# A fused attention and expert kernel: the projection of the batch three ahead moved half a step forward

## The chip, the cores and the metric

The kernel runs on one core of one Trainium2 chip. The metric is the device time of one execution in microseconds (us), lower is better.

## The reference

The input x is 16 batches of 256 tokens of 128 features. Two blocks follow each other, each added to its input:

```python
x = x + _layernorm(attention(_layernorm(x)))     # 16 heads of 8, causal, softmax
x = x + _layernorm(ffn(_layernorm(x)))           # 8 experts, one per token
# attention: Q,K,V = x @ W; softmax(Q K^T / sqrt(8), causal) V, then WO
# ffn: aff = x @ centroids.T; expert = argmax(aff); alpha = sigmoid(aff[expert])
#      y = x + relu(LN_e(x) @ w1_e.T + b1_e) @ w2_e.T + b2_e; out = alpha*y + (1-alpha)*x
```

## The kernel before, in words

The kernel is written by hand for five instruction streams (TensorE is PE, VectorE is DVE, ScalarE is ACT, GpSimd is POOL, and SyncE, called SP, only issues DMAs). Each stream has its own list of instructions in a fixed order, and semaphores order the streams against each other. An instruction that waits holds up all that stands behind it on its stream.

Three phases follow each other: a prologue (to about 38 us), the attention loop over batches (lines 252 to 255, `iterations`, steps 0 to 19 for 16 batches), and an expert phase over 39 tiles of sorted tokens (`tiles`, from about 340 us), which the change doesn't touch. The loop is a software pipeline. In step i these batches are worked on: `new` is i+3, `nxt` is i+1, `t` is i, `old` is i-1, and l2, l3, l4 (on ACT and PE `l2`, `ln`, `last`) are i-2, i-3, i-4. The last steps (i = 16 to 19) have no `t` any more and only drain the pipeline; step 15 has no `nxt`.

What is done for a batch, in its order:

- `normalise_x` (L651, ACT) writes the normalised rows xn; `transpose_x` (L783, PE) turns them into bank MA; `xnT_out` (L564, ACT) copies them out; `project_qk` (L791, PE) makes Q and K in bank MB.
- Q and K are split into three bf16 parts: `high` (L571, ACT) copies MB as bf16, `residue` (L1095, DVE) subtracts it, `middle` (L579, ACT) copies the residue as bf16, `low` (L429, POOL) subtracts that. `parts_out` (L301, SP) sends the parts (384 KB) to a buffer in DRAM, and `parts_in` (L309, SP) fetches them as six DMAs (768 KB) into `qaug` and `kaug`, in the layout that the scores need. A ring of three holds the batches.
- `scores_by_query` (L814, PE) computes the scores of 4 groups of heads (gr) in three portions each (u), into the two halves of bank S in turn, and `maxima` (L1102, DVE, the instruction at L1111) takes each row's maximum out of S. Portion n on PE waits until portion n-2's maximum is taken (the wait on `red`).
- `shift_parts` (L1119, DVE) splits the maxima of half of the heads into bf16 parts, `transpose_shift` (L807, PE) turns them (first half in MA, second in MB), `shift_out` (L584, ACT) copies them to nmT, and `shift` (L324, SP, the DMA at L330) writes them into two rows of qaug, 8 KB.
- In the batch's own step, `scores_near` and `scores_far` (L839, L851, PE) compute the scores again with the shift in them. `scores_near` of group 0 waits for the DMA of `shift(t, 0)`, of group 2 for `shift(t, 1)`. `exp_near` and `exp_far` (L603, L610, ACT) take the exponentials, `select` (L437, POOL) sets the upper triangle to zero, `weigh_values` (L860, PE) multiplies with V, which `project_v` (L799, PE, in MB) and `v_out` (L591, ACT) made.
- Later steps: `o_out`, `transpose_o` (MB), `divide`, `transpose_on`, `project_o`, `y_out`, the layer norm's statistics (`ln_stats`, `ln_aggregate`, `ln_variance` on DVE, `power` on POOL), `add_y`, then `transpose_f`, `affinities_and_ranks` (MB), `choose`, `count`, `place` on DVE, and `scatter` on POOL (L471), which writes the rows by indirect DMA into the experts' table. `add_y` of a batch waits until the scatter of the batch three before has landed (L1198).

MA and MB are each one PSUM bank: the next user on PE waits for the readers of the last one (`take_m`).

The DMAs of SP share one queue. Its order in step i is: `shift(i,1)`, `parts_out(i+2)`, `parts_in(i+2)`, `shift(i+1,0)`, and in some steps a load of expert weights.

Of the kernel before, what the change touches and what calls it, by code (L numbers as in the profile page):

```python
# [51 lines left out]
def sandwich_kernel(nc, x, attn_w, w1x, w2t, b2, cent_t, out):  # L52
# [31 lines left out]
    with ExitStack() as ctx:  # L84
# [209 lines left out]
        def _(sp):  # L294
# [46 lines left out]
            shift(Nth(0), 0)  # L341

            def step(i):
                if b := at(i, 0):
                    shift(b, 1)
                if b := at(i, 2):
                    parts_out(b)
                if b := at(i, 2):
                    parts_in(b)
                if b := at(i, 1):  # L350
                    shift(b, 0)

# [56 lines left out]
        def _(pool):  # L409
# [99 lines left out]
            def step(i):  # L509
                t, ln, last = at(i, 0), at(i, -2), at(i, -4)  # L510
# [5 lines left out]
                if t:  # L516
                    select(t, 2)
                if t:
                    select(t, 3)
                if last:  # L520
                    scatter(last, 0)
                if ln:
                    power(ln, 1)
                if last:
                    scatter(last, 1)
                if ln:
# [3 lines left out]
                if b := at(i, 3):  # L530
                    low(b)
# [29 lines left out]
        def _(act):  # L561
# [109 lines left out]
            middle(Nth(2))  # L671

            def step(i):
# [10 lines left out]
                if new:  # L684
                    normalise_x(new)
                if ln:
                    fT_out(ln)
                if t:
                    exp_near(t, 1)
                    exp_far(t, 1)  # L690
                if new:
                    xnT_out(new)
                if t:
                    exp_near(t, 2)
                if ln or last:
                    affinities_and_ranks_out(i.plus(-3), ln, last)
                if t:
                    exp_far(t, 2)
                if nxt:
                    shift_out(nxt, 0)  # L700
                if nxt:
                    v_out(nxt)
                if t:
                    exp_near(t, 3)
                if old:
                    onT_out(old)
                if t:
                    exp_far(t, 3)
                if new:
                    high(new)  # L710
                if ln:
                    exp_negative(ln)
                if new:
                    middle(new)
# [60 lines left out]
        def _(pe):  # L775
# [176 lines left out]
            def step(i):  # L952
                t, new, nxt, old, l2, ln, last = (at(i, n) for n in (0, 3, 1, -1, -2, -3, -4))

                for gr in range(NG):
# [6 lines left out]
                    if gr == 1 and old:  # L962
                        transpose_o(old)
                    if gr == 2 and i.k == 1:
                        centroid_sums()
                    if gr == 2 and (ln or last):
                        affinities_and_ranks(i.plus(-3), ln, last)
                    if gr == 3 and old:
                        transpose_on(old)
                    if t:  # L970
                        scores_far(t, gr)
                    if nxt:
# [9 lines left out]
                    if gr == 2 and nxt:  # L982
                        transpose_shift(nxt, 0)
                    if gr == 3 and new:
                        project_qk(new)
                    if nxt:
                        scores_by_query(nxt, gr, 2)
                    if gr == 1 and new:
                        transpose_x(new)
# [540 lines left out]
```

## Time and profile before

| what | us |
|---|---|
| median of 3 runs | 438.01 |
| lowest and highest of them | 433.75, 443.32 |
| the profiled execution | 438.63 |
| its span, first to last instruction | 436.9 |

The rows below come from the profiled execution. Times are from its span's start. Step i of the loop is counted from the first `scores_near` of its batch on PE: step 0 begins at 38.52 us, step 1 at 55.45, step 2 at 71.76, step 3 at 91.20, step 4 at 109.03, step 10 at 214.35, step 11 at 231.56, step 14 at 282.05, step 15 at 298.12.

### The profile page before, as it was taken

How to read it: one execution, taken by the hardware profiler on the slowest of the kernel's cores; microseconds unless marked ns; L12 is line 12 of the kernel's file. 1: busy time of each engine (PE TensorE's matmuls, PEld its weight loads, DVE VectorE, ACT ScalarE, POOL GpSimd, SP SyncE). 2: the span in 40 equal slices, each digit the busy share in tenths (PEclk: the TensorE clock that was granted, in tenths of full speed). 3: DMA queues.
4: the chain of work that ended last, by engine and by line, in shares of the span. 5: the costliest groups of instructions: out<-in, count | busy, mean ns of one | idle time of the engine just before them, and what ended most of it. 6: DMA issues, size and time to landing. Idle time of an engine off the chain costs nothing.

```text
span 436.9 us, 11197 instructions
## 1 busy us (share of the span) xinstructions
PE 334.4 (77%) x3642; PEld 268.4 (61%) x3642; DVE 335.6 (77%) x1215; ACT 243.9 (56%) x574; POOL 244.4 (56%) x337
## 2 busy tenths in 40 slices
PE   2348699868978988869897798698620799999950
PEld 1226566656866766647676576485420799999950
DVE  7848777849889799586897898786744399999980
ACT  2204456555765765546667566466410598888850
POOL 3823253625564764654647557547564058888883
PEclk9998989989999999898999999899855699999995
DMA  7662854737536436154363463602004566777710
GB/s 216 107 106 46 113 118 56 110 64 99 86 60 91 93 48 108 51 80 84 49 110 87 52 104 74 90 9 88 14 20 131 160 176 167 205 196 187 217 39 6
DMA packets 34681, 42.78 MB, mean 98 GB/s; under 512 B 5465, under 2 KB 25053, under 8 KB 33088
## 3 DMA queue, kind: packets, MB, share of 16 engines
q1 hardware_dynamic: 31744, 37.43, 44.3%
q0 software_dynamic: 2304, 4.37, 3.1%
q8 instruction: 30, 0.49, 0.5%
q10 hardware_dynamic: 576, 0.27, 0.2%
q14 instruction: 27, 0.22, 0.2%
HBM read 30.59 MB, written 11.66 MB: 97 GB/s over the span
## 4 chain that ended last, share of the span: by engine, by line
PE 44%; DMA 29%; DVE 12%; POOL 5%; issue 5%; ACT 2%; SPq 2%; POOLq 0%; DVEq 0%; ACTq 0%
DMA aug<-nmT 21%; PE ST L848 5%; PE S L1016 4%; PE O L869 4%; PE ST L1016 3%; PE O L1029 3%; PE S L835 3%; PE MB L1029 3%; DVE nmf L1111 3%; PE S L825 2%; PE S L828 2%; DMA qk_parts<-qkp 2%; DMA xs_rows<-pay,pos 2%; PE S L830 2%; DMA aug<-qk_parts 2%
## 5 line engine op out<-in xcount | busy, mean ns | idle before, releaser
L1111 DVE TENSOR_REDUCE nmf<-S 128x2 f32<-128x512 f32 (+1 forms) x192 | 129.5, 681 | 52.3 <-PE S L828 28.3
L441 POOL TENSOR_SCALAR_AFFINE_SELECT p<-p 128x512 f32<-128x512 f32 x64 | 40.9, 638 | 82.5 <-ACT p L608 82.5
L608 ACT ACTIVATE p<-ST 128x1024 f32<-128x1024 f32 x64 | 65.4, 1021 | 26.0 <-PE ST L848 25.2
L848 PE MATMUL ST<-aug 128*128 128x256 bf16 x256 | 40.4, 282 | 30.2 <-DMA aug<-nmT 30.2
L835 PE MATMUL S<-aug 126*128 126x128 bf16 x512 | 51.3, 223 | 0.0
L471 POOL DMA_INDIRECT xs_rows<-pay,pos x32 | 33.1, 1033 | 29.0 <-DVE pos L1270 25.2
L539 POOL DMA_INDIRECT out_x<-vaug,x_all x39 | 42.5, 1090 | 7.8 <-issue 7.5
L848 PEld LDWEIGHTS ST<-aug 128*128 128x128 bf16 x256 | 23.6, 100 | 35.3 <-DMA aug<-nmT 32.6
L445 POOL TENSOR_SCALAR_AFFINE_SELECT p<-p 128x512 f32<-128x512 f32 x64 | 41.2, 644 | 7.1 <-ACT p L612 4.4
L869 PE MATMUL O<-p,vaug 128*32 128x256 f32 x512 | 41.5, 394 | 1.4 <-POOL p L441 1.4
L835 PEld LDWEIGHTS S<-aug 126*128 126x128 bf16 x512 | 40.9, 100 | 2.4
L830 PE MATMUL S<-causal,identb 128*128 128x256 bf16 x128 | 36.4, 284 | 6.9 <-DVE nmf L1111 6.2
L612 ACT ACTIVATE p<-ST 128x512 f32<-128x512 f32 x64 | 38.3, 599 | 0.3
L549 POOL TENSOR_TENSOR rsz<-vez,mhalf 128x1 f32<-128x1 f32 x39 | 22.1, 567 | 24.8 <-DVE vez L1463 24.2
L1434 DVE TENSOR_SCALAR vaug<-ST,w1s 128x128 f32<-128x128 f32 x78 | 23.5, 341 | 11.5 <-PE ST L1016 11.3
L825 PE MATMUL S<-causal,identb 128*128 128x512 bf16 x64 | 25.8, 403 | 7.4 <-DMA aug<-qk_parts 7.4
L435 POOL TENSOR_TENSOR qkp<-res,qkp 128x512 bf16<-128x512 f32 x16 | 18.6, 1163 | 19.7 <-ACT qkp L582 19.7
L1016 PE MATMUL S<-vaug,w1s 128*128 128x128 f32 x156 | 25.5, 288 | 1.6 <-DMA w1s<-in_w1x 0.6
L828 PEld LDWEIGHTS S<-aug 126*128 126x128 bf16 x256 | 20.9, 102 | 9.5 <-issue 1.9
L828 PE MATMUL S<-aug 126*128 126x128 bf16 x256 | 26.3, 227 | 0.0
L873 PE MATMUL O<-p,vaug 128*32 128x128 f32 x512 | 26.2, 275 | 0.0
L577 ACT ACTIVATE qkp<-MB 128x512 bf16<-128x512 f32 x16 | 9.6, 597 | 29.4 <-PE MB L795 29.4
(163 smaller groups left out, 871.7 us busy)
## 6 DMA issues: line engine op xcount, KB each, us to landing
w1s<-in_w1x SPq DMA_DIRECT2D x39, 259.0 KB, 3.2
qk_parts<-qkp SPq DMA_DIRECT2D x16, 384.0 KB, 2.8
aug<-qk_parts SPq DMA_DIRECT2D x32, 192.0 KB
aug<-qk_parts SPq DMA_DIRECT2D x32, 128.0 KB
x_all<-xs_rows SPq DMA_DIRECT2D x39, 67.0 KB, 2.3
aug<-qk_parts SPq DMA_DIRECT2D x32, 64.0 KB
w_tab<-in_w2t SPq DMA_DIRECT2D x8, 256.0 KB, 6.0
out_x<-vaug,x_all POOLq DMA_INDIRECT x39, 3.1
```

The lines of the kernel that those rows point to most:

```text
L441: g.affine_select(out=v, in_=v, compare_op=ALU.is_ge, fill=0.0, base=0, pattern=[[0, 4], [1, P]], channel_multiplier=-1).then_inc(s["sel0" ...
L445: g.affine_select(out=v, in_=v, compare_op=ALU.is_ge, fill=0.0, base=0, pattern=[[0, 4], [1, P]], channel_multiplier=-1).then_inc(s["sel1" ...
L539: g.indirect_dma_start(out=out.rearrange("b t d -> (b t) d"), out_offset=bass.IndirectOffsetOnAxis(ap=xs[:, q, TOK:TOK + 1].bitcast(U32), ...
L608: a.activation(p0[:, gr % 2], ST0[:, :, :], ACT.Exp, scale=SCALE).then_inc(s["exp0"], 1)
L612: a.activation(p1[:, gr % 2], ST1[:, :, :], ACT.Exp, scale=SCALE).then_inc(s["exp1"], 1)
L828: last = mm(bank[:, j * P:(j + 1) * P], q[:, h, 0:P], k[:, h, 0:P], start=False, stop=(j == 3))
L830: mm(bank.rearrange("p (j c n) -> p j c n", j=2, c=2)[:, :, 1], identb[:, :], causal[:, 0:2], start=True, stop=False)
L835: last = mm(bank[:, j * SEQ + kb * P:j * SEQ + (kb + 1) * P], q[:, h, P:SEQ], k[:, h, kb * P:(kb + 1) * P], start=False, stop=(j == 1 and ...
L848: last = mm(ST0[:, j], kaug[:, p, h, 0:P], qaug[:, p, h], start=True, stop=True)
L869: mm(O[32 * j:32 * j + 32, gr // 2, :], vaug[:, p, 0, 4 * gr + j], p0[:, odd, j], start=not odd, stop=False)
L1016: last = mm(hidden(p, c), w1s[:, t.slot(WR), c * P:(c + 1) * P], nT[:, p], start=True, stop=True)
L1111: v.tensor_reduce(dst, S[:, n % 2].rearrange("p (j n) -> p j n", j=k), op=ALU.max, axis=AX_X, negate=True).then_inc(s["red"], 1)
```

## The change

On all five streams the work for `new` is placed earlier:

- SP: `parts_out` is now for i+3 and stands last in the step, behind `shift(i+1,0)`; `parts_in(i+2)` follows `shift(i,1)` directly.
- ACT: `normalise_x` for batch i+4 stands at the end of the step (and one for batch 3 ahead of the loop). `high(new)` stands before `exp_far(t,2)`, `middle(new)` before `exp_near(t,3)`, `v_out(nxt)` just before `exp_far(t,3)`; `affinities_and_ranks_out` is earlier.
- PE: `affinities_and_ranks` moves from group 2 to group 1, `transpose_x` to an earlier place in group 1, `transpose_o` to a later one, `transpose_shift(nxt,0)` and `project_qk(new)` to the front of group 2, `project_v(nxt)` to the end of group 3.
- DVE: `divide` moves behind `shift_parts(nxt,0)`, `residue(new)` ahead of maximum (3,0), `place` and `alphas` are earlier (`place(l4,2)` follows `add_y`), `choose(l3,1)` and `count(l3,0)` are placed anew.
- POOL: `low(new)` stands between `select(t,2)` and `select(t,3)`; `scatter(last,0)` before it, and `scatter(last,1)` ahead of `power(ln,1)`.

```diff
@@ SP
             shift(Nth(0), 0)
+            parts_out(Nth(2))
 
             def step(i):
                 if b := at(i, 0):
                     shift(b, 1)
                 if b := at(i, 2):
-                    parts_out(b)
-                if b := at(i, 2):
                     parts_in(b)
                 if b := at(i, 1):
                     shift(b, 0)
+                if b := at(i, 3):
+                    parts_out(b)
@@ POOL
                 if t:
                     select(t, 2)
+                if last:
+                    scatter(last, 0)
+                if new:
+                    low(new)
                 if t:
                     select(t, 3)
                 if last:
-                    scatter(last, 0)
+                    scatter(last, 1)
                 if ln:
                     power(ln, 1)
-                if last:
-                    scatter(last, 1)
-                if ln:
                     number(ln)
                 if i.k < 2:
                     power_x(i.k + 3)
-                if b := at(i, 3):
-                    low(b)
@@ ACT
             middle(Nth(2))
+            normalise_x(Nth(RING))
...
-                if new:
-                    normalise_x(new)
                 if ln:
                     fT_out(ln)
                 if t:
                     exp_near(t, 1)
-                    exp_far(t, 1)
+                if ln or last:
+                    affinities_and_ranks_out(i.plus(-3), ln, last)
                 if new:
                     xnT_out(new)
                 if t:
+                    exp_far(t, 1)
                     exp_near(t, 2)
-                if ln or last:
-                    affinities_and_ranks_out(i.plus(-3), ln, last)
+                if nxt:
+                    shift_out(nxt, 0)
+                if new:
+                    high(new)
                 if t:
                     exp_far(t, 2)
-                if nxt:
-                    shift_out(nxt, 0)
-                if nxt:
-                    v_out(nxt)
+                if new:
+                    middle(new)
                 if t:
                     exp_near(t, 3)
                 if old:
                     onT_out(old)
+                if nxt:
+                    v_out(nxt)
                 if t:
                     exp_far(t, 3)
-                if new:
-                    high(new)
                 if ln:
                     exp_negative(ln)
-                if new:
-                    middle(new)
+                if b := at(i, 4):
+                    normalise_x(b)
@@ PE
-                    if gr == 1 and old:
-                        transpose_o(old)
-                    if gr == 2 and i.k == 1:
+                    if gr == 1 and i.k == 1:
                         centroid_sums()
-                    if gr == 2 and (ln or last):
+                    if gr == 1 and (ln or last):
                         affinities_and_ranks(i.plus(-3), ln, last)
+                    if gr == 2 and nxt:
+                        transpose_shift(nxt, 0)
+                    if gr == 2 and new:
+                        project_qk(new)
                     if gr == 3 and old:
                         transpose_on(old)
                     if t:
                         scores_far(t, gr)
+                    if gr == 1 and new:
+                        transpose_x(new)
...
-                    if gr == 2 and nxt:
-                        transpose_shift(nxt, 0)
-                    if gr == 3 and new:
-                        project_qk(new)
+                    if gr == 1 and old:
+                        transpose_o(old)
                     if nxt:
                         scores_by_query(nxt, gr, 2)
-                    if gr == 1 and new:
-                        transpose_x(new)
-                    if gr == 2 and nxt:
+                    if gr == 3 and nxt:
                         project_v(nxt)
@@ DVE
+                if l4:
+                    alphas(l4, 0)
                 if nxt:
                     maxima_and_stats(i, nxt, 1, 1)
                 if l2:
                     ln_variance(l2, 0)
                 if l4:
-                    alphas(l4, 0)
+                    alphas(l4, 1)
...
+                if nxt:
+                    maxima_and_stats(i, nxt, 1, 2)
+                if l4:
+                    place(l4, 0)
+                if nxt:
+                    shift_parts(nxt, 0)
                 if old:
                     divide(old)
-                if l4:
-                    alphas(l4, 1)
-                if nxt:
-                    maxima_and_stats(i, nxt, 1, 2)
                 if nxt:
                     maxima_and_stats(i, nxt, 2, 0)
-                    shift_parts(nxt, 0)
+                if l4:
+                    place(l4, 1)
+                if l3:
+                    choose(l3, 0)
                 if l2:
                     add_y(l2)
+                if l4:
+                    place(l4, 2)
...
+                if new:
+                    residue(new)
                 if nxt:
                     maxima_and_stats(i, nxt, 3, 0)
...
-                if new:
-                    residue(new)
+                if l3:
+                    count(l3, 0)
                 if nxt:
                     shift_parts(nxt, 1)
```

## Rows read from the trace of the kernel before

**Rows 1.** Busy time by stretch: PE, PEld, DVE, ACT, POOL; PE clock, DMA share, GB/s.

```profile
55.45:282.05 226.60, 194.71 (x2392) 148.69 (x2393) 185.12 (x587) 138.54 (x297) 125.76 (x173) 0.97 0.49 82
176.50:196.33 19.83, 15.98 (x186) 12.34 (x187) 14.29 (x47) 11.01 (x24) 11.29 (x16) 0.93 0.41 68
214.35:231.56 17.21, 14.72 (x186) 11.26 (x187) 15.19 (x52) 11.45 (x25) 10.93 (x15) 1.00 0.48 83
282.05:298.12 16.07, 14.92 (x181) 11.48 (x182) 12.30 (x40) 9.08 (x19) 7.38 (x12) 0.90 0.08 24
```

**Rows 2.** Waits of the whole run: total us, times, longest.

```profile
PE ST L848 <- DMA aug<-nmT: 30.2, 14, 3.9
```

**Rows 3.** Timeline of SP in step 10: start us, us.

```profile
216.97 0.62 SPq L330 DMA_DIRECT2D aug<-nmT  x1
218.00 0.39 SPq L307 DMA_DIRECT2D qk_parts<-qkp  x1
221.01 0.31 SPq L318 DMA_DIRECT2D aug<-qk_parts  x1
...
224.44 0.62 SPq L330 DMA_DIRECT2D aug<-nmT  x1
```

**Rows 4.** The chain of waits at the same place.

```profile
224.44 7.07 DMA aug<-nmT
```

**Rows 5.** Timeline of PE, end of step 10 and start of step 11.

```profile
228.96 0.39 PE L835 MATMUL S<-aug 126*128 126x128 bf16 x4
231.56 0.61 PE L848 MATMUL ST<-aug 128*128 128x256 bf16 x4 [2.21 <-DMA aug<-nmT]
```

**Rows 6.** Timeline of DVE in step 10: divide, maxima, residue.

```profile
221.50 0.42 DVE L1138 TENSOR_TENSOR on<-MB,rden 128x256 f32<-128x256 f32 x1
...
221.91 1.27 DVE L1111 TENSOR_REDUCE nmf<-S 128x2 f32<-128x512 f32 x2
...
228.09 0.68 DVE L1111 TENSOR_REDUCE nmf<-S 128x4 f32<-128x512 f32 x1
...
230.12 0.67 DVE L1099 TENSOR_TENSOR res<-MB,qkp 128x512 f32<-128x512 f32 x1
```

**Rows 7.** Timeline of ACT in step 10: normalise_x, v_out, middle.

```profile
217.85 0.87 ACT L658 ACTIVATE xn<-x_all,nbx,rsx 128x128 f32<-128x128 f32 x2
...
225.09 0.45 ACT L600 ACTIVATE vaug<-MB 128x128 f32<-128x128 f32 x2 [0.67 <-PE MB L802]
...
230.82 0.63 ACT L582 ACTIVATE qkp<-res 128x512 bf16<-128x512 f32 x1 [1.08 <-DVE res L1099]
```

**Rows 8.** Groups of instructions, steps 4 to 13: busy us, mean ns.

```profile
L608 ACT ACTIVATE p<-ST 128x1024 f32<-128x1024 f32 x40 | 40.9, 1021 | 9.2 <-PE ST L848 8.7
...
L1187 DVE TENSOR_SCALAR pay<-mv_x 128x2 f32<-128x2 f32 x10 | 5.3, 528 | 0.0
...
L1188 DVE TENSOR_SCALAR ve_x<-mv_x 128x2 f32<-128x2 f32 x10 | 1.6, 155 | 0.0
```

**Rows 9.** Timeline of DVE and SP in step 0.

```profile
39.75 0.16 DVE L1084 SCALAR_TENSOR_TENSOR nbx<-mvx,rsx 128x6 f32<-128x6 f32 x1
...
44.30 0.31 SPq L318 DMA_DIRECT2D aug<-qk_parts  x1
```

**Rows 10.** The chain of waits in steps 16 and 17.

```profile
313.95 0.62 DVE pay L1200 x2
...
316.22 0.74 issue
316.96 1.04 POOL xs_rows L471
318.03 1.04 POOL pay L454
319.08 0.20 issue
...
321.72 0.63 DVE pay L1200 x2
```

More of the change, by code:

```diff
@@ L509, in step @@
             def step(i):
-                t, ln, last = at(i, 0), at(i, -2), at(i, -4)
+                t, new, ln, last = at(i, 0), at(i, 3), at(i, -2), at(i, -4)
                 if t:
@@ L1325, in step @@
                 if l4:
-                    alphas(l4, 0)
+                    alphas(l4, 1)
+                if i.k == 1:
+                    centre_centroids()
+                if nxt:
[4 more added lines that the diff above has]
+                    shift_parts(nxt, 0)
                 if old:
                     divide(old)
-                if l4:
-                    alphas(l4, 1)
-                if nxt:
-                    maxima_and_stats(i, nxt, 1, 2)
                 if nxt:
                     maxima_and_stats(i, nxt, 2, 0)
-                    shift_parts(nxt, 0)
+                if l4:
+                    place(l4, 1)
+                if l3:
+                    choose(l3, 0)
                 if l2:
                     add_y(l2)
+                if l4:
+                    place(l4, 2)
                 if nxt:
@@ L1341, in step @@
                     ln_stats(l2, 1)
-                if l4:
-                    place(l4, 0)
-                if i.k == 1:
-                    centre_centroids()
                 if l3:
-                    choose(l3, 0)
+                    choose(l3, 1)
                     ln_shift(l3)
@@ L1352, in step @@
                     maxima_and_stats(i, nxt, 2, 2)
-                if l4:
-                    place(l4, 1)
                 if l3:
-                    choose(l3, 1)
                     scale_max(l3)
@@ L1359, in step @@
                     ln_variance(l2, 1)
+                if new:
+                    residue(new)
                 if nxt:
                     maxima_and_stats(i, nxt, 3, 0)
-                if l4:
-                    place(l4, 2)
                 if l3:
@@ L1376, in step @@
                 if l3:
-                    count(l3, 0)
                     count(l3, 1)
```

## The prediction

> **What bounds the kernel now.** I read the busy time by stretch first, then the waits, then one step in the timeline of each engine, and last the chain of waits. The loop's steps 1 to 13 (55.45 to 282.05 us) take 226.6 us, 17.43 each. In them PE is busy 194.7 and DVE 185.1, which is 15.0 and 14.2 a step, so neither fills its step; but the engines are near enough to each other that removing one wait uncovers the next [rows 1]. PE's largest wait is that of the first `scores_near` of a step for the DMA that writes the shift: 30.2 us in 14 times [rows 2]. Step 10 shows why it is late. `shift(i,1)` is issued 2.6 us into the step (216.97 against 214.35), `parts_out` at 218.00, and `parts_in` stands behind its landing until 221.01 [rows 3]. `shift(i+1,0)` is issued at 224.44, is 8 KB, and takes 7.07 us, since the 768 KB of `parts_in` are ahead of it [rows 3, 4]. PE has done its own step at 228.96 + 0.39 = 229.35, 15.0 us after the start, and stands still for 2.21 until 231.56 [rows 5]. So in such a step PE and DVE have some 15 us of work and the DMA queue sets 17.2. Where a transfer runs late the step grows one for one: the step of 176.50 took 19.83 [rows 1].
>
> **The DMA side of the change.** `parts_out(i+2)` goes a step back, so `parts_in` follows `shift(i,1)` directly. From the first issue of `parts_in` to the landing of the shift behind it is 231.51 - 221.01 = 10.5 us [rows 3, 4]. ACT reaches `shift_out(t,1)` later than now, because `v_out` (0.45), `exp_far(3)` (some 0.5) and `normalise_x` (0.87) now stand between the step's start and `exp_near(0)` [rows 7], 1.5 to 1.8 together; I put the shift's issue at 4.2 us into the step instead of 2.6. `parts_in` then starts at about 4.8, and the shift has landed at 4.8 + 10.5 = 15.3. PE needs it at 16 to 17. The wait is hidden with 1 to 2 us to spare, and a slow transfer like that of the 19.83 us step is mostly absorbed. `parts_out` itself (one DMA, the same count as before) takes 3.0 us to land (218.00 to 221.01) [rows 3]; issued near 0.5 of the next step, after POOL's `low`, it lands at 3.5, ahead of the point (4.8) where `parts_in` waits for it. The shift it stands ahead of, `shift(i,1)`, is issued at 4.2 and needed at 7.
>
> The Trainium skill ("DMA: Bandwidth & Descriptors", Queues, rings and completion order) says that each DMA engine takes descriptors in ring order but that completion isn't first-in first-out for one issuing engine. Were a small DMA free to overtake, the wait before the change would not be behind `parts_in` at all and moving it would give nothing in this term; the 7.07 us of an 8 KB transfer speak for the ring order [rows 4].
>
> **What is late next: DVE's stretch between two maxima.** PE may run only two portions ahead of DVE, so the order on DVE decides. Before, from the start of maximum (1,2) to that of (3,0) DVE needs 228.09 - 221.91 = 6.18 us without a gap [rows 6]. Into this stretch the change puts `divide` (reciprocal and product, start to start some 0.8, of which the product is the 0.42 at 221.50) and `residue` (0.67) [rows 6]: 7.6, with a small `place` 7.7. Portion (1,2) is ready at about 7.9 into the step (before 7.56, by 221.91 - 214.35 [rows 5, 6]): PE has `affinities_and_ranks` and `transpose_x` ahead of it, and the former waits for `fT_out` on ACT, some 0.4. The residue is then ready at 15.6. ACT has `middle` (0.63) [rows 7] and `exp_near(3)` (1.02) [rows 8] behind it, and the next step's `scores_near` waits for that exponential: 15.6 + 0.6 + 1.0 + 0.1 = 17.3. That is the upper bound of the step by this order. PE's own stops beside it (`transpose_shift` waits for `shift_parts` some 0.6, `project_qk` for `divide` another 0.6, since both now stand early in group 2) lie inside it.
>
> The lower bound comes from DVE instructions that are stretched now. The same small operation takes 0.528 at L1187 and 0.155 at L1188 [rows 8]; in the stretch counted above four kinds do this (variance, one-hot, `add_y`, the cast of the shift), together about 1.5 us. They are the ones that meet a select on POOL. In the new order POOL has its selects of group 2 done before the variance comes, so part of this goes: 15.8 if all goes. I take 16.7, a little nearer to the order's sum than to the other end, because the one-hot still meets a select.
>
> The Trainium skill ("SBUF — State Buffer", Who interferes with whom) has VectorE and GpSimd share a port pair under an exclusive lock held for a whole instruction. By that rule the loss depends on which instructions meet, not on their number; with none meeting the step would be 15.8 and the whole about 412, with all of them 17.3 and about 431. The trace agrees in kind: 0.528 beside 0.155 [rows 8].
>
> **The sum, against the profiled execution's 438.6 us.**
>
> - Start of the loop: `normalise_x(3)` now stands ahead of `exp_near(0,0)` on ACT and waits for DVE's bias at 39.75 [rows 9], and takes 0.87 [rows 7, 9], so that exponential and `shift(0,1)` behind it come some 1.7 later, the DMA at 42.5; `parts_in(2)`, whose parts have by then landed, still starts at 43.2 instead of 44.30 [rows 9]. Step 1 begins 1.1 us sooner.
> - Steps 1 to 13: 13 x (17.43 - 16.7) = 9.5 us less [rows 1]. Of the 30.2 us of waits this keeps a third; the rest turns into waits of PE for DVE and ACT. In it is the clock: in the step of 176.50 to 196.33 the granted clock is 0.93 and PE's same 186 instructions take 15.98 instead of 14.72 [rows 1]. It falls to the lower of its two levels (1.2 of 2.4 GHz) after such a stop; with stops under 1 us I count none.
> - Step 14 (16.07 us, clock 0.90 [rows 1]) loses its slow start but is held by DVE: 0.3 less.
> - The drain (steps 15 to 19). The chain goes from `add_y` to its next 321.72 - 313.95 = 7.77 us later: `add_y`, statistics and choosing up to `pos`, scatter 1.04, `power` 1.04 with 0.20 behind it, second scatter, landing [rows 10]. `place(l4,2)` now follows `add_y` directly, which lets the first scatter start 1.4 sooner (313.95 + 0.62 + 0.16 + 0.74 = 315.5 against 316.96), and `power` no longer stands between the scatters, 1.24. That is 2.7 for the link shown. The one before has only the 1.2 of `power`; in the last one the chain needs `power` itself, which now stands behind two scatters, so that of the 1.4 only 0.2 is kept. Together 4.1. Between 0 (if y's own path ends last) and 5.5 (two full links).
> - The expert phase and the work ahead of 38.5 us: nothing changes, 0.
>
> 438.6 - 1.1 - 9.5 - 0.3 - 4.1 = 423.6 us. The profiled execution is 0.6 above the median of the runs, so the two stand for the same kernel; single runs of it spread by 2%.
>
> What I cost at nothing: the earlier `alphas` and `count` (DVE waits there for PE anyway, in groups 0 and 1), the move of `transpose_x`, and SP's extra `parts_out` ahead of the loop (its three us are inside step 0).
>
> **Rivals.**
>
> *PE becomes the bound.* If DVE runs less tightly than I count, the step falls to PE's own 15.0 [rows 5] and some 0.3: 15.3. Then 13 x 2.13 = 27.7, and 438.6 - 1.1 - 27.7 - 0.3 - 4.1 = 405. For it: PE is busy 14.72 in a clean step. Against: DVE is busy 15.19 there [rows 1]. Chance 0.12.
>
> *The stretched instructions stay, or the gain is only the late transfers.* Step 17.2: 13 x 0.23 = 3, and 438.6 - 1.1 - 3 - 0.3 - 4.1 = 430. For it: the sum in order gives 17.3. Chance 0.22.
>
> *The fetch doesn't come sooner (the change doesn't do what it says).* `low(new)` now stands behind `scatter(last,0)` on POOL, which waits for `place` on DVE; if `parts_out` lands after 7 us of the step, `parts_in` starts when it does now. Then only the start's slack and the drain count: 438.6 - 4.1 = 434.5. Against: POOL is busy 10.93 of 17.21 [rows 1]. Chance 0.08.
>
> *Slower: ACT's order closes the loop.* ACT is in order, and `middle(new)` waits for DVE ahead of `exp_near(3)`, `v_out` waits for the last product of PE's step ahead of `exp_far(3)`, and both stand ahead of the next `exp_near(0)`. `exp_near(0)` starts 2.0 into the step (0.2 until the product is there, then the 1.5 to 1.8 from above) and ends at 3.0; PE asks for it (group 1) at 3.5. If `v_out` starts over 0.5 us later than I have it, every us more on ACT is a us more on the step. With 1 us over my upper bound the step is 18.3: 13 x 0.87 = 11.3 more, 438.6 - 1.1 + 11.3 - 4.1 = 444.7. It decides from a step of 17.8 on, where the drain's gain is used up. Against: ACT is busy 11.45 of 17.21 [rows 1]. Chance 0.10.
>
> **How the numbers follow.** The forecast (step 15.8 to 17.0, which is 412 to 428) has 0.48, the rivals 0.12, 0.22, 0.08 and 0.10. The range runs from 411 to 435: below it is the rival with PE as the bound, above it the slower one. A measurement of this kernel can tell about 2% from no change, that is 429 on the one side and 447 on the other. The forecast and PE's rival fall under 429, and of the 430 case a little less than half: 0.70 faster. Same: the rest of it, the late fetch and most of the slower case: 0.25. Slower by over 2%: 0.05.
>
> **What would show it.** In the changed profile: PE's wait at `scores_near` for the DMA of nmT falls from 30.2 us to under 5; SP issues `parts_in` 4 to 5.5 us into a step, not 6.7; new waits of PE at `transpose_shift` for DVE and at `project_qk` for `divide`, 0.3 to 0.8 each; ACT's `middle` directly behind DVE's `residue`, with `exp_near(3)` behind it; the granted clock 0.98 and more over steps 1 to 13, none as long as 19.83; in the drain the two scatters side by side and `add_y` to `add_y` 5 to 5.5 us. Wrong would be: a wait of `scores_near` for the DMA of over 1 us a step, a step with PE at 15.3, or one over 17.8.

## The result, and the profile after

| what | before | after |
|---|---|---|
| median, us | 436.28 (4 runs) | 413.51 (4 runs) |
| lowest and highest | 433.75, 443.32 | 412.54, 414.44 |
| the profiled execution | 438.63 | 413.59 |
| its span | 436.9 | 411.8 |

The ratio is 0.9496, with a 95% interval of 0.9429 to 0.9563: the change makes the kernel 5% faster. From profile to profile it gives 25.0 us, where 15.0 were forecast. The time lies inside the range, 10 us below the forecast. Some executions are slower as a whole, at a lower granted clock (the profiled one of before, 443.32 before, 448.62 of fetch_late, 496.48 of both_moves), and by the others alone, as in all ratios here, the change is worth 21.9 us rather than 25.0.

Busy time by stretch after the change (columns as in [rows 1]): steps 1 to 13, step 9, and step 14.

```profile
52.78:259.81 207.03, 191.67 (x2392) 146.63 (x2393) 176.54 (x599) 131.57 (x294) 122.94 (x172) 1.00 0.52 92
196.40:212.48 16.08, 14.98 (x186) 11.49 (x187) 13.74 (x48) 10.39 (x25) 9.99 (x15) 1.00 0.50 84
259.81:275.01 15.20, 13.91 (x183) 10.48 (x180) 13.54 (x47) 8.62 (x19) 8.83 (x13) 1.00 0.10 29
```

The 13 steps take 19.57 us less [rows 1], and the granted clock is 1.00 in all of them, instead of 0.97. They are alike now: steps 3 to 12 take 16.1 each, where [rows 1] show one of 19.83 and one of 17.21 (step 13, the first without `new`, takes 15.15). The start of step 1 came forward from 55.45 to 52.78 (2.67), step 14 is 0.87 shorter, and from the start of step 15 to the expert phase's first normalisation on ACT it is 40.10 instead of 41.75 (1.65). These four are 24.8 of the 25.0.

Waits: PE's for the DMA of the shift over the whole run, and PE's two largest in 84 to 244 us (ten steps).

```profile
PE ST L849 <- DMA aug<-nmT: 0.5, 1, 0.5
PE MB L796 <- DVE on L1139: 4.2, 10, 0.4
PE MA L811 <- DVE nmp L1129: 4.1, 10, 0.4
```

The wait of [rows 2] went from 30.2 us in 14 times to 0.5 in 1. What came instead is 0.42 and 0.41 a step. SP's timeline, from step 9 (196.40) to step 10 (212.48), answers to [rows 3]:

```profile
199.99 0.62 SPq L330 DMA_DIRECT2D aug<-nmT  x1
200.70 0.38 SPq L318 DMA_DIRECT2D aug<-qk_parts  x1
...
205.88 0.62 SPq L330 DMA_DIRECT2D aug<-nmT  x1
212.70 0.39 SPq L307 DMA_DIRECT2D qk_parts<-qkp  x1
216.07 0.62 SPq L330 DMA_DIRECT2D aug<-nmT  x1
```

`shift(9,1)` is issued 3.6 us into its step, `parts_in` 4.3, and `parts_out` 0.2 into the next step. PE no longer stands at the end of a step (compare [rows 5]):

```profile
211.42 0.28 PE L831 MATMUL S<-causal,identb 128*128 128x256 bf16 x1
...
211.76 0.66 PE L803 MATMUL MB<-wat,xnT 128*128 128x128 f32 x4
212.48 0.60 PE L849 MATMUL ST<-aug 128*128 128x256 bf16 x4
```

DVE's stretch of the same step, from maximum (1,2) to the residue (compare [rows 6]):

```profile
204.08 0.69 DVE L1112 TENSOR_REDUCE nmf<-S 128x2 f32<-128x512 f32 x1 [0.87 <-PE S L836]
...
207.70 0.69 DVE L1112 TENSOR_REDUCE nmf<-S 128x2 f32<-128x512 f32 x1 [0.43 <-PE S L836]
...
208.70 0.38 DVE L1215 SCALAR_TENSOR_TENSOR hotk<-aff,amax,down 128x8 f32<-128x8 f32 x2
...
209.88 0.25 DVE L1188 TENSOR_SCALAR pay<-mv_x 128x2 f32<-128x2 f32 x1
...
210.09 0.68 DVE L1100 TENSOR_TENSOR res<-MB,qkp 128x512 f32<-128x512 f32 x1
210.69 0.68 DVE L1112 TENSOR_REDUCE nmf<-S 128x4 f32<-128x512 f32 x1
...
211.96 0.75 DVE L1222 TENSOR_TENSOR hot<-down,key 128x16 bf16<-128x16 f32 x1
```

The maximum starts 7.68 into the step, and the residue is done 6.69 later, at 210.77, which is 14.37. Of the 6.69, 0.43 is DVE standing still for PE's portion (2,1) at 207.70, so 6.26 is its own work. ACT follows it without a gap, and `exp_near(3)` ends at 212.33, 0.15 before PE begins the next step:

```profile
210.80 0.63 ACT L582 ACTIVATE qkp<-res 128x512 bf16<-128x512 f32 x1 [2.57 <-DVE res L1100]
211.33 1.00 ACT L608 ACTIVATE p<-ST 128x1024 f32<-128x1024 f32 x1
```

### The profile page after: what moved, and what is told of

The parts are those of the page before. It is cut to its first block, busy times and chain, and to the rows that moved or that the text cites. A ratio compares the mean times of both kernels' runs of the same rounds, so it can differ in the third digit from the quotient of the medians.

```text
span 411.8 us, 11210 instructions
## 1 busy us (share of the span) xinstructions
PE 331.5 (80%) x3642; PEld 265.7 (65%) x3642; DVE 326.3 (79%) x1215; ACT 237.3 (58%) x574; POOL 241.3 (59%) x337
## 4 chain that ended last, share of the span: by engine, by line
PE 44%; DVE 21%; issue 12%; POOL 8%; DMA 7%; ACT 4%; SPq 2%; POOLq 0%; DVEq 0%; ACTq 0%
PE S L836 5%; DVE nmf L1112 5%; PE O L870 4%; PE MB L796 4%; POOL out_x L539 3%; PE ST L849 3%; PE S L831 3%; PE MB L884 2%; PE ST L858 2%; DVE res L1100 2%; DMA aug<-qk_parts 2%; PE O L874 2%; PE S L1017 2%; POOL rsz L549 2%; PE S L829 2%
## 5 line engine op out<-in xcount | busy, mean ns | idle before, releaser
L446 POOL TENSOR_SCALAR_AFFINE_SELECT p<-p 128x512 f32<-128x512 f32 x64 | 40.7, 636 | 42.9 <-ACT p L612 42.4
L442 POOL TENSOR_SCALAR_AFFINE_SELECT p<-p 128x512 f32<-128x512 f32 x64 | 40.5, 633 | 28.7 <-ACT p L608 28.6
L836 PE MATMUL S<-aug 126*128 126x128 bf16 x512 | 50.6, 221 | 0.0
L836 PEld LDWEIGHTS S<-aug 126*128 126x128 bf16 x512 | 40.3, 99 | 2.1
L472 POOL DMA_INDIRECT xs_rows<-pay,pos x32 | 32.2, 1005 | 14.2 <-DVE pay L1257 6.5
L849 PE MATMUL ST<-aug 128*128 128x256 bf16 x256 | 38.5, 272 | 1.9 <-ACT p L608 0.7
L582 ACT ACTIVATE qkp<-res 128x512 bf16<-128x512 f32 x16 | 10.1, 630 | 35.0 <-DVE res L1100 35.0
L829 PEld LDWEIGHTS S<-aug 126*128 126x128 bf16 x256 | 20.3, 99 | 9.0 <-issue 1.1
L849 PEld LDWEIGHTS ST<-aug 128*128 128x128 bf16 x256 | 21.9, 97 | 5.9 <-issue 2.2
L796 PE MATMUL MB<-xnT,wat 128*128 128x256 f32 x64 | 20.8, 454 | 6.1 <-DVE on L1139 5.0
```

The source lines that it names most:

```text
L442: g.affine_select(out=v, in_=v, compare_op=ALU.is_ge, fill=0.0, base=0, pattern=[[0, 4], [1, P]], channel_multiplier=-1).then_inc(s["sel0" ...
L446: g.affine_select(out=v, in_=v, compare_op=ALU.is_ge, fill=0.0, base=0, pattern=[[0, 4], [1, P]], channel_multiplier=-1).then_inc(s["sel1" ...
L796: last = mm(MB[:, w * SEQ:(w + 1) * SEQ], wat[:, w], xnT[:, b.slot(RING)], start=True, stop=True)
L836: last = mm(bank[:, j * SEQ + kb * P:j * SEQ + (kb + 1) * P], q[:, h, P:SEQ], k[:, h, kb * P:(kb + 1) * P], start=False, stop=(j == 1 and ...
L849: last = mm(ST0[:, j], kaug[:, p, h, 0:P], qaug[:, p, h], start=True, stop=True)
```

## The experiments

My theory after the result: the queue no longer sets the step. The step is set by the chain residue, `middle`, `exp_near(3)`, next `scores_near`, with PE's own order a few tenths behind it, and it is shorter than forecast because DVE's stretched instructions are nearly gone. Rivals: SP's new order alone does it; PE is the bound; DVE's whole sum is.

**fetch_late.** The new kernel with SP's old order.

```diff
@@ SP
             shift(Nth(0), 0)
-            parts_out(Nth(2))
...
                 if b := at(i, 2):
+                    parts_out(b)
+                if b := at(i, 2):
                     parts_in(b)
                 if b := at(i, 1):
                     shift(b, 0)
-                if b := at(i, 3):
-                    parts_out(b)
```

> The changed kernel with SP's order of the kernel before: shift(i,1), parts_out(i+2), parts_in(i+2), shift(i+1,0). All other engines as changed. Theory (the earlier send is what takes the DMA out of the path): the shift(i,1) is issued 3.6 us into a step of the changed kernel; parts_out behind it needs 3.0 to land, parts_in and the shift behind it 10.5, so the next step can't begin before 17.9 instead of 16.1: 13 x 1.8 = 23 us more, near 437, with PE's wait for the DMA of nmT back at 1.5 to 2 us a step. Rival (the engines' order alone made the gain, the DMA would fit anyway): under 2 us more, 413 to 415.

438.21 us (433.60 to 448.62), a ratio of 1.0 (0.9917 to 1.0082). The whole gain is gone with SP's order alone, and the wait for the DMA is back. Its waits of the whole run:

```profile
PE ST L848 <- DMA aug<-nmT: 19.0, 14, 4.3
SPq L318 <- DMA qk_parts<-qkp: 34.2, 14, 2.8
```

**send_alone.** The kernel before with SP's new order (the diff of SP in the section on the change), the engines' orders as they were.

> The kernel before with SP's new order alone: parts_out(i+3) at the end of step i, one ahead of the loop. Theory (the projection has to be sooner as well): low ends 3.6 us into the next step, SP waits for it, shift(i,1) and parts_in stand behind that wait, and parts_in starts at the same place as before: no change within 1%, 434 to 440. Rival (the order of the DMAs is all): the wait of 30 us falls by more than half, 415 to 420.

437.15 us (435.14 to 438.69), ratio 1.0008 (0.9955 to 1.0061). The waits of the whole run, and a step's end on SP:

```profile
PE ST L849 <- DMA aug<-nmT: 26.1, 17, 3.1
SPq L307 <- POOL qkp L436: 132.4, 16, 10.0
```

```profile
228.72 0.39 SPq L307 DMA_DIRECT2D qk_parts<-qkp  x1
229.20 0.62 SPq L330 DMA_DIRECT2D aug<-nmT  x1
231.49 0.29 SPq L318 DMA_DIRECT2D aug<-qk_parts  x1
```

In the old order of the engines `low` is late, so SP waits in front of `parts_out` (132.4 us in all, against 94.3 in the new kernel), and the next shift stands behind it. Neither half does anything alone: what pays is that the parts are ready half a step sooner and that they are sent before the fetch is due.

**residue_late.** Takes the residue back behind maximum (3,0), which makes the chain to the next step 0.6 longer and leaves DVE's sum as it is.

```diff
@@ DVE
-                if new:
-                    residue(new)
                 if nxt:
                     maxima_and_stats(i, nxt, 3, 0)
+                if new:
+                    residue(new)
```

> The changed kernel with DVE's residue(new) behind maximum (3,0) instead of ahead of it. Theory (the step ends by residue, middle, exp_near(3), next scores_near): the residue is 0.6 later, PE's next step begins 0.4 to 0.6 later, 14 steps: 6 to 8 us more, 419 to 421. Rival (DVE's sum sets the step, or the path over maximum (3,0) and portion (3,2) does): no change, or 1 to 3 us less.

423.34 us (422.07 to 425.08), ratio 0.9697 (0.9649 to 0.9746): 9.8 us more than the new kernel, where 6 to 8 were expected (7.9 of it is in steps 1 to 13), and the step is 16.69, longer by 0.61. The residue starts 0.6 later, and so does all that hangs on it: the waits of PE in 84 to 244 us, and the start of a step.

```profile
PE ST L849 <- ACT p L608: 7.7, 10, 0.8
```

```profile
203.64 0.60 PE L849 MATMUL ST<-aug 128*128 128x256 bf16 x4 [0.80 <-ACT p L608]
```

The chain is shown: one maximum in front of the residue costs its own length in every step.

**middle_late.** ACT's `middle` behind `exp_near(3)`, which takes its 0.63 out of the chain.

```diff
@@ ACT
-                if new:
-                    middle(new)
                 if t:
                     exp_near(t, 3)
+                if new:
+                    middle(new)
```

> The changed kernel with ACT's middle(new) behind exp_near(3) instead of ahead of it. Theory: the path over ACT goes, and the one over maximum (3,0), portion (3,2) and project_v, which ends 0.22 us sooner in the trace, sets the step: 2 to 3 us less, 410 to 412. Rival (the ACT order doesn't matter, or low and so the send come too late): 413 to 416.

413.92 us (413.37 to 414.85), ratio 0.9481: no gain, where I expected 2 to 4 us. The step is 16.05. PE goes from `project_v` straight into the next step as before, so behind the chain lies a second path, shorter by under 0.1. It starts at the residue too: maximum (3,0) behind it, then portion (3,2) on PE, ahead of which PE is idle for 0.08 in the new kernel, then `project_v`. And `exp_near(0)` moved from 1.67 to 1.87 into the step, since `v_out` waits behind the later `middle`.

**select_small.** Does GpSimd's select stretch what is left, and is DVE's sum the bound? The selects cover one head of four; the mask of the others is left out.

```diff
@@ POOL, select
-                v = p0[:, gr % 2, :, 0:P]
+                v = p0[:, gr % 2, 0:1, 0:P]
...
-                                pattern=[[0, 4], [1, P]], channel_multiplier=-1).then_inc(s["sel0"], 1)
+                                pattern=[[0, 1], [1, P]], channel_multiplier=-1).then_inc(s["sel0"], 1)
```

(the same for p1)

> The changed kernel with the mask set for one head of four only (POOL's two selects work on 128 columns instead of 512; the mask of the other heads is left out). Theory (DVE's stretched instructions are those that meet a select on POOL, and what is left of them in the changed kernel lies where DVE has slack): the one-hot comparison (L1222, 0.75) and the shift's difference (L1129, 0.37) fall to 0.16 to 0.2, the step stays within 0.2 us of 16.09: 409 to 414. Rival 1 (the stretch comes from something else): both stay as they are. Rival 2 (DVE's sum sets the step): it falls by the 1 us that DVE gains, 398 to 401.

412.23 us (411.22 to 414.16), ratio 0.9481; the step is 16.06. Groups of instructions in 84 to 244 us, here and then in the new kernel:

```profile
L1222 DVE TENSOR_TENSOR hot<-down,key 128x16 bf16<-128x16 f32 x9 | 6.8, 753 | 0.0
L1129 DVE TENSOR_TENSOR nmp<-nmf,nmp 128x16 bf16<-128x16 f32 x20 | 4.4, 218 | 0.7
```

```profile
L1222 DVE TENSOR_TENSOR hot<-down,key 128x16 bf16<-128x16 f32 x9 | 6.7, 745 | 0.0
L1129 DVE TENSOR_TENSOR nmp<-nmf,nmp 128x16 bf16<-128x16 f32 x20 | 7.5, 373 | 0.7
```

The second split of the maxima was stretched by a select and no longer is. The one-hot at L1222 stays: what it meets is `low`, as GpSimd's timeline of the new kernel shows (the one-hot runs from 211.96 to 212.71, `low` ends at 212.68).

```profile
211.52 1.16 POOL L436 TENSOR_TENSOR qkp<-res,qkp 128x512 bf16<-128x512 f32 x1 [1.35 <-ACT qkp L582]
```

I had put this one-hot down to a select; that half of the theory fell. DVE's busy time in 84 to 244 us goes from 135.64 to 133.03, 0.26 a step, most of it in the second `shift_parts`, behind the residue, and the step gains only 0.03, so DVE's sum is not the bound. The test is weaker than planned, since 1 us was to go.

**qk_later.** Takes PE's stop at `project_qk` away by placing it behind portion (2,1).

```diff
@@ PE
                     if gr == 2 and nxt:
                         transpose_shift(nxt, 0)
-                    if gr == 2 and new:
-                        project_qk(new)
...
                     if nxt:
                         scores_by_query(nxt, gr, 1)
+                    if gr == 2 and new:
+                        project_qk(new)
```

> The changed kernel with PE's project_qk(new) one place later, behind portion (2,1) instead of ahead of scores_far(2). Theory (inside a step project_qk, waiting 0.4 for divide and then taking 1.0, holds portion (2,1), and DVE waits 0.43 for that on the way to the residue): DVE's wait goes, the step is 0.3 to 0.45 shorter, 13 steps: 4 to 6 us less, 407.5 to 409.5. Rival (the step is set elsewhere, or high and the residue come too late): 413 to 416.

411.15 us (410.45 to 412.74), ratio 0.9457; the step is 15.99, 0.10 less, where 0.3 to 0.45 was expected. PE's waits in 84 to 244 us:

```profile
PE MA L811 <- DVE nmp L1129: 4.1, 10, 0.4
PE S L831 <- DVE nmf L1112: 1.6, 9, 0.2
```

The 0.42 for `divide` is gone, and with it DVE's 0.43 for portion (2,1). But DVE, now ahead, is in the other part of the one-hot (`hotk`) while a select runs on GpSimd (206.08 to 206.71):

```profile
205.92 0.81 DVE L1215 SCALAR_TENSOR_TENSOR hotk<-aff,amax,down 128x8 f32<-128x8 f32 x2
```

This pair took 0.38 in the new kernel. From the start of maximum (1,2) at 201.83 to the end of the residue at 208.41 it is 6.58 instead of 6.69, so of the 0.43 only 0.11 is kept, which is the step's gain. PE's new wait of 0.2 is at the last portion, (3,2).

**drain_add_y_first.** In the steps from 16 on DVE does `add_y` ahead of `place(l4,0)` and `divide`.

```diff
@@ DVE
+                if l2 and i.k >= B:
+                    add_y(l2)
                 if l4:
                     place(l4, 0)
...
-                if l2:
+                if l2 and i.k < B:
                     add_y(l2)
```

> The changed kernel with DVE's add_y ahead of place(l4,0) and divide in steps 16 and later, where there are no maxima. Theory (the drain gained 1.7 and not 4.1 us because add_y of step 16 stands behind place, which waits for the ranks, and behind divide): add_y comes 2.5 to 3 us sooner in step 16, and the expert phase begins 1 to 2.6 us sooner: 411 to 412.5. Rival (the y path of batch 15 or POOL sets the drain): under 0.5 us.

413.04 us (412.84 to 414.39), the same as the new kernel. `add_y` of step 16 starts at 289.92 instead of 292.63, 2.7 sooner. The next one gains only 0.9 of that (298.54 before the edit), and the expert phase begins at 315.09 instead of 315.11:

```profile
289.92 0.61 DVE L1201 SCALAR_TENSOR_TENSOR pay<-yb,rs_y,x_all 128x128 f32<-128x128 f32 x2 [2.50 <-POOL rs_y L453]
...
297.61 0.62 DVE L1201 SCALAR_TENSOR_TENSOR pay<-yb,rs_y,x_all 128x128 f32<-128x128 f32 x2 [1.28 <-POOL rs_y L453]
```

The first `add_y` doesn't set it. That y's own path of batch 15 does (divide, projection, statistics, `rs_y`), as the rival says, fits the 1.28 that the next `add_y` waits for `rs_y`.

**normalise_mid.** On top of middle_late, `normalise_x` stands behind `fT_out`, for batch i+3, and none ahead of the loop; so `exp_near(0)` no longer stands behind it.

```diff
@@ ACT
-            normalise_x(Nth(RING))
...
                 if ln:
                     fT_out(ln)
+                if new:
+                    normalise_x(new)
...
-                if b := at(i, 4):
-                    normalise_x(b)
```

> middle_late with ACT's normalise_x(i+3) behind fT_out(i-3) instead of at the end of the step before. Theory (with middle behind exp_near(3) PE ends a step 0.2 sooner but loses it in groups 0 and 1, because v_out, exp_far(3), normalise_x (0.8) hold exp_near(0) and y_out, for which PE waits): those waits go, the step is 15.8 to 15.9 instead of 16.05: 2 to 3 us less, 410.5 to 412. Rival (that part is PE's own work, or the move only shifts the wait to exp_near(1)): 413 to 415.

410.59 us (409.91 to 411.96), ratio 0.9442 (0.9362 to 0.9522); step 15.85, as expected. Beside middle_late this is 0.20 a step: ACT's place at the step's start did hold the loop, by tenths.

**pool_busy.** The term that I had mis-sized, put back: two selects on a scratch buffer on GpSimd behind `scatter(last,0)` (they only add work), where the variance comes on DVE.

```diff
@@ POOL
                 if last:
                     scatter(last, 0)
+                if t and new:
+                    for n in (0, 1):
+                        g.affine_select(out=junk[:, 2 * (i.k % 2) + n], in_=ident[:, :].unsqueeze(1).to_broadcast([P, 4, P]),
+                                        compare_op=ALU.is_ge, fill=0.0, base=0, pattern=[[0, 4], [1, P]],
+                                        channel_multiplier=-1).then_inc(s["junk"], 1)
                 if new:
                     low(new)
```

> The changed kernel with two more selects on POOL (128x512, onto a scratch tile, 0.6 us each) behind scatter(last,0), where POOL stands idle for 1.3 us before low; nothing waits for them. They run beside DVE's scale_max, variance and residue. Theory (the step came out shorter than forecast because DVE's instructions between maximum (1,2) and the residue no longer meet POOL's): the variance (L1188 of the changed kernel, 0.23 there, 0.53 before) is stretched again, the residue ends 0.4 to 0.7 later and so does the step, 16.5 to 16.8: 418 to 422. Rival (POOL's work doesn't touch DVE, or the residue isn't on the path): 412.5 to 415.

426.35 us (425.31 to 426.85), ratio 0.9812 (0.9755 to 0.9869): 12.8 us more than the new kernel, where 418 to 422 was expected, and 17.35 a step. Its timelines of POOL, of DVE and of PE in one step:

```profile
221.53 1.24 POOL L524 TENSOR_SCALAR_AFFINE_SELECT junk<-ident 128x512 f32<-128x512 f32 x2
```

```profile
215.44 0.69 DVE L1118 TENSOR_REDUCE nmf<-S 128x2 f32<-128x512 f32 x1 [0.87 <-PE S L842]
...
221.37 0.83 DVE L1194 TENSOR_SCALAR pay<-mv_x 128x2 f32<-128x2 f32 x1
...
222.19 0.60 DVE L1196 TENSOR_SCALAR ve_x<-mv_x 128x2 f32<-128x2 f32 x1
222.70 0.68 DVE L1106 TENSOR_TENSOR res<-MB,qkp 128x512 f32<-128x512 f32 x1
```

```profile
224.03 0.28 PE L837 MATMUL S<-causal,identb 128*128 128x256 bf16 x1 [1.34 <-DVE nmf L1118]
```

From the start of maximum (1,2) to the end of the residue it is 222.70 + 0.68 - 215.44 = 7.94 instead of 6.69. That is 1.25 more, and the step grew by 1.26: a stretched instruction ahead of the residue costs its full length. PE's wait of 1.34 is at portion (3,2) for maximum (3,0), so this run lengthens the second path of middle_late together with the chain over `middle`; residue_late, where maximum (3,0) comes sooner and the residue later, is the run that lengthens the chain alone. The Trainium skill ("SBUF — State Buffer", Who interferes with whom) has the shared port pair of VectorE and GpSimd as an exclusive lock; the trace agrees, with two steps of the variance of 0.83 and 0.60, of a kind that takes 0.155 at L1188 [rows 8], and they end at 222.20 and 222.79, where the two selects end at about 222.15 (half of the 1.24) and at 222.77.

**both_moves.** normalise_mid and qk_later together.

> normalise_mid and qk_later together. Theory: the two act on different parts of the step (groups 0 and 1 on ACT, group 2 on PE), so their gains of 0.24 and 0.10 us a step add up: step 15.7 to 15.8, 408 to 409.5. Rival (each uncovers the same next limit): as normalise_mid, 410 to 411.

405.72 us (403.88 to 407.30), ratio 0.9324 (0.9245 to 0.9403), less than the 408 to 409.5 expected. The step is 15.57, 0.51 less than in the new kernel, where the two alone (with middle_late's) gave 0.23 and 0.10. That they give more together fits paths of nearly equal length, none of which gives much until all are shortened. In 84 to 244 us PE is busy 152.94 of 160, and its waits are these:

```profile
PE MA L810 <- DVE nmp L1128: 4.1, 10, 0.4
PE S L830 <- DVE nmf L1111: 1.6, 9, 0.2
```

14.88 busy, 0.41 and some 0.16 are 15.45 of the 15.57. PE is nearly full here, but both waits are for DVE, and DVE in turn stands 0.88 a step for PE's portion (1,2): the bound is the loop through both, not PE alone. This version beats both kernels.

**drain_y_first.** The new kernel with the y path first in the steps from 16 on: `transpose_o` ahead of `affinities_and_ranks` on PE, `divide` and `add_y` ahead of `place(l4,0)` on DVE.

```diff
@@ PE
+                    if gr == 1 and old and i.k >= B:
+                        transpose_o(old)
...
-                    if gr == 1 and old:
+                    if gr == 1 and old and i.k < B:
                         transpose_o(old)
@@ DVE
+                if old and i.k >= B:
+                    divide(old)
+                if l2 and i.k >= B:
+                    add_y(l2)
                 if l4:
                     place(l4, 0)
...
-                if old:
+                if old and i.k < B:
                     divide(old)
...
-                if l2:
+                if l2 and i.k < B:
                     add_y(l2)
```

> The changed kernel with another order in steps 16 and later: transpose_o ahead of affinities_and_ranks on PE, divide and add_y ahead of place on DVE. Theory (what holds the drain is the path of batch 15's y: transpose_o waits for bank MB behind the affinities, then divide, transpose_on, project_o, y_out, power): transpose_on of batch 15 comes 1 to 1.5 us sooner and so does the expert phase: 411.5 to 412.8. Rival (the ranks of batch 12, now later, or the scatters on POOL hold it): 413 to 414.

412.33 us (411.14 to 413.33), ratio 0.9496 (0.9435 to 0.9557). `transpose_on` of batch 15 starts at 290.87 instead of 292.71, and the drain from step 15's start to the expert phase takes 38.42 instead of 40.10. In the total it is 1.2, within what runs of one kernel differ by. Nor is the 1.7 shown to be the edit's: pool_busy, whose order from step 16 on is the new kernel's, takes 38.55 (290.11 to 328.66), and middle_late 39.83.

**all_moves.** both_moves with drain_y_first's order.

> both_moves with the order of drain_y_first in steps 16 and later. Theory (the step and the drain don't touch each other): the step stays at 15.57 us as in both_moves, the stretch from the start of step 15 to the first normalise of the expert phase is 1.5 to 1.8 us shorter than there (38.84), 404 to 406. Rival (the drain's gain is used up by the later q and k order or the copy of the rows): 406.5 to 407.5.

408.63 us (6 runs, 407.07 to 411.89), ratio 0.9427 (0.9356 to 0.9498): a miss, no better than both_moves, and the two intervals overlap. Two things show. In the profile `add_y` of step 16 comes at 286.39, in both_moves at 286.45: `transpose_o`, and `divide` behind it, waits for ACT's copy of O there (PE stands 1.4 for it), so going first gains nothing. But `place`, now behind the later affinities, starts at 287.93 instead of 284.39, and its scatters 1.4 later; the next `add_y` stands for their landing.

```profile
286.39 0.61 DVE L1202 SCALAR_TENSOR_TENSOR pay<-yb,rs_y,x_all 128x128 f32<-128x128 f32 x2
287.93 0.17 DVE L1265 TENSOR_TENSOR posw<-rank,hot 128x16 f32<-128x16 f32 x1 [0.93 <-ACT rank L643]
...
294.96 0.61 DVE L1202 SCALAR_TENSOR_TENSOR pay<-yb,rs_y,x_all 128x128 f32<-128x128 f32 x2 [3.61 <-DMA xs_rows<-pay,pos]
```

In both_moves that one starts at 292.35. And the steady step is 15.71 instead of 15.57, though the edit touches none of its instructions. The two traces part at ACT's `o_out`, which starts 3.37 into step 9 instead of 3.00 although PE's last product before it comes at the same time; what holds it no run tells. The profiled execution took 411.89, so its step may not be that of the others. That stays open.

## Why the prediction was right, and where its sizes were off

**Right: the wait, and what it was for.** The fetch was late because `parts_out` stood in front of it, and the shift behind it; both went, at the points named (`parts_in` at 4.3 against 4.8, the shift at 3.6 against 4.2, `parts_out` at 0.2 of the next step against 0.5). fetch_late gives the whole gain back, and send_alone shows that the earlier send alone is worth nothing. The clock is 1.00, and no step is long. Of the two new stops of PE, put at 0.6 each, 0.41 and 0.42 came. The rival that the fetch doesn't come sooner is excluded by SP's timeline.

**Right: what is late next.** residue, `middle`, `exp_near(3)`, next step: residue_late and pool_busy lengthen this chain by 0.6 and 1.25, and the step follows by 0.61 and 1.26. The path over maximum (3,0) is as long to within 0.1 (middle_late), which the prediction didn't see. The slower rival, ACT's order, had the right place: `exp_near(0)` starts at 1.67 instead of the 2.0 assumed, and the 0.3 in hand held. normalise_mid shows that it costs some 0.2 a step, not 1.

**The term that was mis-sized: "I take 16.7 ... because the one-hot still meets a select".** The mean step is 15.93, the steady one 16.08. The bounds, 15.8 with all stretched instructions gone and 17.3 with none, held. (That pool_busy ends at 17.35 is chance: it adds work that the bound didn't have.) The one-hot of that sentence is the part of `choose` that stands in the stretch, `hotk`. First before, in steps 4 to 13, then after, in 84 to 244 us:

```profile
L1214 DVE SCALAR_TENSOR_TENSOR hotk<-aff,amax,down 128x8 f32<-128x8 f32 x20 | 8.2, 447 | 0.0
...
L1200 DVE SCALAR_TENSOR_TENSOR pay<-yb,rs_y,x_all 128x128 f32<-128x128 f32 x20 | 9.9, 532 | 0.0
```

```profile
L1188 DVE TENSOR_SCALAR pay<-mv_x 128x2 f32<-128x2 f32 x10 | 2.3, 230 | 0.0
...
L1215 DVE SCALAR_TENSOR_TENSOR hotk<-aff,amax,down 128x8 f32<-128x8 f32 x20 | 3.8, 230 | 0.0
...
L1201 DVE SCALAR_TENSOR_TENSOR pay<-yb,rs_y,x_all 128x128 f32<-128x128 f32 x20 | 6.1, 345 | 0.0
```

`hotk` hardly meets a select any more (447 to 230 ns, two a step), the variance fell from 528 [rows 8] to 230, and `add_y` from 532 to 345. The comparison at L1222 is stretched (157 ns at L1221 before, 745 after), but by `low`, and it stands behind the residue, where it costs nothing. So DVE's own work in the stretch is 6.26 instead of the 7.7 in order: of the "about 1.5 us" 1.4 is gone, nearly the lower bound's case. In return DVE stands 0.43 for portion (2,1), behind `project_qk` on PE. This the prediction had put at nothing ("PE's own stops ... lie inside it"). The sum is 7.68 (7.9 forecast) + 6.26 + 0.43 + 1.71 from the residue's end to the next step = 16.08.

The 13 steps gave 10.1 us more than forecast. The others, start, step 14 and drain, gave 1.6 and 0.6 more and 2.5 less, and nearly cancel, so the 10.0 between 423.6 and 413.6 lie in this term. The 226.60 us of the 13 steps before isn't fixed either: fetch_late and send_alone, no faster than before, take 222.28 and 222.41, beside which the 207.03 is 15 us less and not 19.57.

**The start** gave 2.67 instead of 1.1. SP's timeline has `parts_in(2)` at 42.86 (43.2 forecast) and `shift(1,0)` at 46.56 instead of 47.61, 1.05 sooner, as said. But that shift lands 52.78 - 46.56 = 6.2 us after its issue, where it took 55.45 - 47.61 = 7.8: the transfers were shorter by 1.6, which I had taken as fixed. That is luck of the execution: in drain_add_y_first and drain_y_first, whose order is the same up to step 15, the shift is issued at 46.58 and 46.59 and step 1 begins at 53.55 and 54.73, 7.0 and 8.1 later. In all three SP issues the loads of `w_tab`, `cent` and `b_tab` from 53 us on instead of at 48.27 right behind the shift, so their move doesn't make the transfer short.

**Step 14**: 0.87 instead of 0.3; its clock is now 1.00 instead of 0.90 [rows 1], which I hadn't counted.

**The drain: "together 4.1"** gave 1.65. The link itself shortened about as said, `add_y` to `add_y` 298.54 - 292.63 = 5.91 where it was 7.77 [rows 10], against 5.1 forecast. But the first of them comes 17.6 us after step 15's start (275.01), where it was 313.95 - 298.12 = 15.8: on DVE `place(l4,0)` and `divide` now stand ahead of it, and each waits for PE and ACT. My working took the link's gain and left out what the new order puts in front of its first end. How much that costs isn't shown: drain_add_y_first moves this `add_y` by 2.7 for nothing, and in pool_busy, with the new order, it comes 15.8 after step 15's start (305.91 - 290.11). So the path over this `add_y` isn't the one that ends last. That y's path of batch 15 is (the prediction's "0 if y's own path ends last") fits, but drain_y_first's 1.7 is no more than the drain differs by between runs of one order, so it stays open.

**PE as the bound (15.3)** was nearly reached: PE's 14.98 and its two stops make 15.80 of 16.08. both_moves gets to 15.57, with PE still waiting for DVE.

## What to carry to other kernels

A pipeline of in-order streams is moved as a whole: the sender's new order alone gave 1.0008, the engines' new order alone 1.0, both together 0.95. When one wait is taken out of a loop with several engines near 90% busy, write down the order up to the next step's first instruction, and count only what stands in front of it; an instruction behind the last link costs nothing, whatever it is stretched to. After each move look again at what now runs beside what: qk_later took a wait of 0.43 away and lost 0.3 of it to an instruction that came to stand beside a select. And where single edits give nothing (middle_late), try them together: three edits worth 0.04, 0.20 and 0.10 a step gave 0.51.

## What the runs showed of the hardware

I hadn't expected that 1.24 us of GpSimd work, placed badly, costs 1.26 us of every step, 1.12 of it (start to start) through two DVE instructions of 128x2 elements. What is stretched and what isn't: the variance (128x2, SBUF to SBUF) went from 0.16 to 0.83, the comparison at L1222 from 0.16 to 0.75, `hotk` (128x8, a pair) from 0.38 to 0.81. A maximum, which reads PSUM, took 0.65 to 0.69 beside a select or away from one in every profile, the product of `divide`, with one input in PSUM, 0.42, and the pair of statistics at L1170 0.48 beside a select. The residue stood beside none for more than 0.06. That the cheapest place for a select is beside such instructions follows from this, but no run tries it.
